# The first attention and routing of a two-layer cross-attention kernel: from steps of 512 tokens to single tiles, and from gathered to scattered expert rows

## The reference

```python
x = x + tanh(g_xattn[0]) * xattn0(layernorm(x), ctx)   # 16 heads of 128, rmsnorm on q and k, softmax over 64 keys
x = x + tanh(g_ffn[0])   * ffn0(layernorm(x))          # 64 experts, 8 per token, plus a shared expert
x = x + tanh(g_xattn[1]) * xattn1(layernorm(x), ctx)   # 16 heads of 16, per-head layernorm on q and k, 48+16 keys
x = x + tanh(g_ffn[1])   * ffn1(layernorm(x))          # 8 experts computed densely, top 2 weighted, plus shared
```

```python
scores = sigmoid(x @ router_weight.T); sc = scores + e_bias
# 8 groups of 8 experts: sum of the two best of each group, best 4 groups kept, best 8 experts in them
topk_w = scores[topk_idx]; topk_w = 2.5 * topk_w / topk_w.sum()
pos = (number of earlier tokens, in order, that chose the same expert)   # kept where pos < 128
buf[e, pos] = x[token]                                  # 64 blocks of 128 rows
y = (silu(buf @ w_gate) * (buf @ w_up)) @ w_down        # 88 inner values
out[token] += y * topk_w
```

## Time and profile before

| | us |
|---|---|
| median of 3 runs (lowest, highest) | 1350.04 (1349.48, 1351.49) |
| profiled execution, its own time | 1348.91 |
| its span, first to last instruction | 1347.2 |
| busy PE, PEld, DVE | 1040.4, 860.9, 714.3 |
| busy ACT, POOL | 428.9, 296.6 |
| mean granted TensorE clock | 0.833 |

### The profile page before, as it was taken

How to read it: one execution, slowest core, us unless ns; L and a number is a source line. 1 busy time by engine, 2 the same in 40 slices (tenths; PEclk the granted TensorE clock), 3 DMA queues, 4 the chain that set the end, 5 groups by cost and what they waited for, 6 DMA issues and landing times. The chain is left out here.

```text
span 1347.2 us, 16347 instructions
## 1 busy us (share of the span) xinstructions
PE 1040.4 (77%) x5301; PEld 860.9 (64%) x5301; DVE 714.3 (53%) x1663; ACT 428.9 (32%) x789; POOL 296.6 (22%) x231
## 2 busy tenths in 40 slices
PE   5989989999766500866775447878879999999997
PEld 3857858678554300755665226564757989899896
DVE  6367586674768896222222488575865424242221
ACT  4555365544623100111111032323252232322321
POOL 0414223133000001788787120120200000000000
PEclk9999999999877655877778666767676999999999
DMA  7004000000001140788886620000000000000001
GB/s 264 3 0 136 1 1 1 0 1 1 0 0 39 42 108 22 168 182 175 170 175 113 191 107 1 2 0 0 0 0 0 1 1 0 0 0 0 0 0 63
DMA packets 59495, 66.39 MB, mean 49 GB/s; under 512 B 5565, under 2 KB 56247, under 8 KB 58679
## 3 DMA queue, kind: packets, MB, share of 16 engines
q1 hardware_dynamic: 45796, 46.52, 11.1%
q0 software_dynamic: 12288, 18.88, 7.9%
q10 hardware_dynamic: 1363, 0.37, 0.1%
HBM read 48.16 MB, written 17.56 MB: 49 GB/s over the span
## 5 line engine op out<-in xcount | busy, mean ns | idle before, releaser
L1978 PE MATMUL bank<-gu_hi,xnT_split 128*128 128x352 f32 x640 | 159.4, 329 | 0.0
L476 POOL TENSOR_TENSOR q_lo<-soft,q_hi 128x512 fp32r<-128x512 f32 x64 | 93.1, 1455 | 238.0 <-ACT soft L1338 237.8
L1978 PEld LDWEIGHTS bank<-gu_hi,xnT_split 128*128 128x128 f32 x640 | 113.4, 191 | 1.0 <-issue 0.7
L487 POOL DMA_INDIRECT xg<-table,src_now x64 | 63.9, 999 | 217.6 <-DVE src_now L948 198.5
L497 POOL DMA_INDIRECT acc<-y,dst_now x64 | 102.2, 1596 | 26.7 <-issue 20.6
L1978 PE MATMUL bank<-gu_lo,xnT_split 128*128 128x352 f32 x320 | 104.2, 326 | 0.0
L1208 DVE SCALAR_TENSOR_TENSOR soft<-sg,combine_w,bank 128x176 f32<-128x176 f32 x160 | 56.5, 394 | 88.1 <-PE bank L1978 82.3
L1997 PE MATMUL bank<-dn,attnT 128*128 128x256 f32 x448 | 102.1, 387 | 0.0
L1997 PEld LDWEIGHTS bank<-dn,attnT 128*128 128x128 f32 x448 | 86.1, 195 | 11.5
L728 DVE COPY qT<-bank 128x512 f32<-128x512 f32 x64 | 44.2, 690 | 89.3 <-PE bank L1683 88.2
L1536 ACT ACTIVATE sg<-bank 128x352 f32<-128x352 f32 x80 | 37.1, 464 | 153.0 <-PE bank L1978 153.0
(11 more groups left out here) (255 smaller groups left out, 2165.4 us busy)
## 6 DMA issues: line engine op xcount, KB each, us to landing
w_gu<-in_L_ffn_w_gu SPq DMA_DIRECT2D x32, 352.0 KB
w_dn<-in_L_ffn_w_down SPq DMA_DIRECT2D x32, 176.0 KB
acc<-zeros SPq DMA_DIRECT2D x2, 2176.0 KB, 12.0
acc_rows<-acc SPq DMA_DIRECT2D x8, 512.0 KB, 4.9
gu<-in_L_gu SPq DMA_DIRECT2D x1, 3520.0 KB, 13.3
table<-xw SPq DMA_DIRECT2D x4, 640.0 KB
wo<-in_L_xattn_Wo SPq DMA_DIRECT2D x2, 1024.0 KB, 15.7
wq<-in_L_xattn_Wq SPq DMA_DIRECT2D x1, 2048.0 KB, 18.0
```

Of the source, the lines that this page charges most:

```text
L476: pool.tensor_tensor(q2_lo[:, h % 3, :], q2[h % 2], q2_hi[:, h % 3, :], ALU.subtract).then_inc(q2_split, 1)
L487: pool.indirect_dma_start(xg[:, q, e, :], None, table, bass.IndirectOffsetOnAxis(ap=src_now[:, q, e:e + 1], axis=0)).then_inc(xg_loaded[q] ...
L1978: mm = pe.matmul(b[:, 0:2 * F1], v[:, c, j * P:(j + 1) * P], w[:, c, p, o, :], start=(n == 0), stop=(n == len(terms) - 1))
```

## The change

The first layer's attention becomes a loop of 18 slots, unrolled, one tile of 128 tokens to a slot. The order of fills of all four PSUM rings is written out by name (`first_stage_turns`, class `Turns`), and each engine looks its position up there.

Queries are now projected with the tile stationary and 512 columns of `wq` moving, and are used for their norms alone: ACT squares each head's 128 columns in PSUM with a sum (`query_norms`). Scores come from the normed tile and a matrix per context batch, a = Wq^T-folded keys: for each head PE multiplies `wqT` by `kT` (`fold`), and ACT lays the result in `a_sk`. Key norms are also squares with sums on ACT (`keys_in`). `raw` holds one tile. Routing runs inside the loop on pairs of tiles (`choose`), five slots behind; the position of a token in its expert's block is a count made by PE with a triangular matrix (`place`); the two instructions' results are row numbers in a DRAM table of 64 x 128 rows. POOL sends each token's row (256 values, 64 weights, its own number) with eight indirect stores a tile (`send_rows`). Blank rows are written to the whole table at the start, with numbers of spare rows in the accumulators. The shared expert runs after the loop. The slot search and the gathers are gone: SP loads blocks with plain DMAs (`load_rows`), and the adding scatter takes its indices from the loaded rows.

In the second attention the centring is done once, on weights and biases (`centre_weights`, placed before the last round of experts), and weight and bias of the per-head norm are applied by ACT in the copies that follow the transposes (`queries1_in`, `keys1_in`). Loads, waits and names follow. The core of the diff, cut:

```diff
+            sp.dma_start(wq[:], a["L0_xattn_Wq"]...).then_inc(wq_loaded, 16)
+            sp.dma_start(wqT[:], a["L0_xattn_WqT"]).then_inc(wqT_loaded, 16)
             sp.dma_start(wvT[:], a["L0_xattn_WvT"]).then_inc(wv_loaded, 16)
+            sp.dma_start(wvo[:], a["L0_xattn_Wo"]...).then_inc(wo_loaded, 16)
             sp.dma_start(x[:, G:NT, :], x_d[:, G:NT, :]).then_inc(x_rest_loaded, 16)
+            for n in range(4):
+                each = E0 // 4
+                sp.dma_start(table_d[:, n * each:(n + 1) * each, :], blank[:].unsqueeze(1).to_broadcast(
+                    [P, each, ROW])).then_inc(blank_stored, 16)
+            for n in range(NA):
+                sp.dma_start(acc[n]..., blank[:, 0:DIM]...).then_inc(zeroed, 16)
+            for g in range(1, NG):
+                sp.wait_ge(t_ring.full, t_turn.at["ctxV", g - 1] + 1)
+                sp.dma_start(ctx_rows[:], ctx_d[g * P:(g + 1) * P, :]).then_inc(ctx_loaded, 16)
...
+            sp.wait_ge(row_stored, 16 * K0 * NT)
+            for q in range(4):
+                load_rows(0, q)
...
                     sp.wait_ge(y_full, 4 * i + q - 3)
                     load_experts(i, q)
+                    for n in range(NA):
+                        sp.wait_ge(acc_added[n], 16 * (4 * i + q - 3))
+                    load_rows(i, q)
```

```diff
+            def send_rows(b):                                  # POOL
+                if b >= 2:
+                    pool.wait_ge(row_stored, 16 * K0 * 2 * (b - 1))
...
+                pool.wait_ge(slots_ready, b + 1)
+                if b == 0:
+                    pool.wait_ge(blank_stored, 16 * 4)
+                for j in range(2):
+                    for k in range(K0):
+                        pool.indirect_dma_start(table, bass.IndirectOffsetOnAxis(ap=slots[:, b % 2, j, k:k + 1], axis=0),
+                                                rows[:, b % 2, j, :], None, bounds_check=E0 * CAP - 1,
+                                                oob_is_err=False).then_inc(row_stored, 16)
-            def gather(i, q):
-                for e in range(2):
-                    pool.indirect_dma_start(xg[:, q, e, :], None, table, bass.IndirectOffsetOnAxis(
-                        ap=src_now[:, q, e:e + 1], axis=0)).then_inc(xg_loaded[q], 16)
```

```diff
+            def slot(i):                                       # DVE
+                if i >= 6 and i % 2 == 0:
+                    place((i - 6) // 2)
+                if i >= 5 and i % 2:
+                    choose((i - 5) // 2)
+                roots(i)
+                if i >= 2:
+                    apply2(i - 2)
+                if i + 1 < NT:
+                    apply1(i + 1)
+                if i < NT:
+                    soft_front(i)
+                if i + 1 < NT:
+                    split1(i + 1)
+                if 1 <= i <= NT:
+                    residual1(i - 1)
+                if i % G == 0 and i // G + 1 < NG:
+                    key_norm(i // G + 1)
+                if i < NT:
+                    soft_back(i)
```

```diff
+            def keys_in(g):                                    # ACT
+                for n in range(4):
+                    b = q_turn.read(act, ("keys", g, n))
+                    act.activation(ksb[:, 4 * n:4 * n + 4, :], b[:]..., ACT.Copy).then_inc(keys_copied, 1)
+                    act.wait_ge(keys_copied, 4 * g + n + 1)
+                    for k in range(4):
+                        v = b[:, k * D0:(k + 1) * D0]
+                        ins = act.activation(v, v, ACT.Square, accum_out=kstat[:, 0, 4 * n + k:4 * n + k + 1])
+                    ins.then_inc(q_ring.free, 1)
+            def slot(i):
+                g = i // G
+                if 1 <= i < NT:
+                    query_norms(i)                             # 16 squares with a sum, like the above
+                if i >= 3:
+                    scores_in1(i - 3)
+                if g and i < NT and i % G == 1:
+                    values_in(g, range(4, 8))
+                if 1 <= i <= NT:
+                    attn_in(i - 1)
+                if i + 1 < NT:
+                    tokens_in(i + 1)
+                if i < NT:
+                    exponential1(i)
+                if i == 0:
+                    product_in()
+                    values_in(0, range(8))
+                if i < NT and g and i % G == 0:
+                    values_in(g, range(2, 4))
+                if g + 1 < NG:
+                    if i % G == 0:
+                        context_in(g + 1)
+                        keys_in(g + 1)
+                    elif i % G == 1:
+                        keysT_in(g + 1)
+                    elif i % G == 2:
+                        fold_in(g + 1, 0)
+                    else:
+                        fold_in(g + 1, 1)
+                        values_in(g + 1, range(2))
+                if i >= 2:
+                    rows_in(i - 2)
```

```diff
+            def slot(i):                                       # PE
+                if 1 <= i < NT:
+                    queries(i)
+                if i >= 3:
+                    route(i - 3)
+                if g and i < NT and i % G == 1:
+                    values(g, range(4, 8))
+                if 1 <= i <= NT:
+                    transpose_attn1(i - 1)
+                if i < NT:
+                    scores1_(i)
+                if i + 1 < NT:
+                    transpose1(i + 1)
+                if 1 <= i <= NT:
+                    output1(i - 1)
+                if i >= 5 and i % 2:
+                    place((i - 5) // 2)
...
-                for h in range(H0):
-                    b = qr.fill(pe)
-                    terms = [(w, v, c) for c in range(C) for w, v in (
-                        (wq_hi, xnT_top), (wq_hi, xnT_rest), (wq_lo, xnT_top))]
```

More of the change, by code:

```diff
@@ L179, in flamingo @@
[L179 to L189, removed]
@@ L490, in scatter @@
+            for b in range(NT // 2):
+                send_rows(b)
+            pool.drain().then_inc(done1["pool"], 1)
             def scatter(i, q):
@@ L827, in _, with two @@
[L827 to L846 removed]
+            def two(v):
+                return v.rearrange("p (j e) -> p j e", j=2)
@@ L954, in experts @@
+            shared_product(0)
+            shared_product(1)
+            place(last)
+            for i in range(NG):
+                if i >= 2:
+                    shared_product(i)
+                shared_out(i)
+            dve.drain().then_inc(done1["dve"], 1)
+            CH1 = ch.base + ch.k
+            for e in done1.values():
+                dve.wait_ge(e, 1)
+            sl = Chain(dve, slot_chain)
+            def experts(i):
                 qr.at(Q3, 4, i)
                 for q in range(4):
-                    if not (last and q):
-                        stage_source(i + (q + 3) // 4, (q + 3) % 4)
@@ L1377, in _ @@
+            for i in range(NT + 2):
+                slot(i)
+            scores_in1(NT - 1)
+            for i in range(NG):
+                if i >= 2:
+                    act.wait_ge(o_ring.full, o_turn.at["shared", G * (i - 2) + G - 1] + 1)
+                act.activation(sh_g[:, i % 2, :], q_turn.read(act, ("gate", i))[0:I0, :], ACT.Silu).then_inc(q_ring.free, 1)
             act.drain().then_inc(done1["act"], 1)
@@ new lines, in scores1_ @@
+            def scores1_(t):
+                if t % 2 == 0:
+                    t_turn.emptied(pe, ("fold", t // G, 1, 3))
+                for n in range(2):
+                    b = s_turn.fill(pe, ("scores", t, n))
+                    for c in range(C):
+                        mm = pe.matmul(b[:], xnT1[:, t % 2, c, :], a_sk[:, (t // 2) % 3, c, n * 512:(n + 1) * 512],
+                                       start=(c == 0), stop=(c == C - 1))
+                    mm.then_inc(s_ring.full, 1)
@@ new lines, in shared_out @@
+            def shared_out(i):
+                s_turn.emptied(pe, ("up", i))
+                for j in range(G):
+                    b = o_turn.fill(pe, ("shared", G * i + j))
+                    pe.matmul(b[:, 0:DIM], sh_h[:, i % 2, j * P:(j + 1) * P], sh_dn[:], start=True,
+                              stop=True).then_inc(o_ring.full, 1)
+            pe.wait_ge(ident_ready, 1)
+            context_in(0)
+            pe.wait_ge(wk_loaded, 16)
+            keys(0)
+            transpose1(0)
```

1368 lines of the change are left out of this document (653 added, 715 removed).

## The result

The changed kernel takes **1376.38 us** (median of 4 runs, 1374.01 to 1385.0), the kernel before 1349.76 in the same comparison: the ratio is 1.0207, with a 95% interval from 1.0162 to 1.0252. It is slower, by 1.6 to 2.5%; I had forecast 1297 with a range of 1235 to 1348. The profiled execution took 1374.01 us with a span of 1372.3.

What follows compares the result with a forecast made beforehand. Bounds: PE to about 335 us, not PE from 335 to 531 (softmax, routing, slot search), POOL in the experts. 1347.2 - 40 (experts ending earlier) - 13 (second attention) = 1294 span, plus 1.7 and 1.1: 1297 us, range 1235 to 1348.

Steps and rivals of the forecast that it cites:

- Then the tail is POOL's: After the slots end at 433 us, POOL's stores of blocks 5, 6 and 7 remain, 21 us a block, 63 us.
- First rows: Start of the experts' stage: first rows at 518 us, where the kernel before has them at about 536.
- Rival (3): POOL's stores are held up or as dear as scatters, 1.93 us: 30 us more in the tail, 1327; chance 0.13.
- A group of four tiles: Expert-free first attention loop: four slots take 103 us, of which PE works 75.
- the 15 us that I had added for clocks and semaphores: Added to 503 us for lower clocks in gaps and semaphores between engines, giving 518 us before the experts.
- The context: Loop's start: next context's load, behind blank rows and zeros on SP's queue, lands at 77 us; 15 us lost.
- Squares with sums: ACT's sixteen squares a tile in the loop, taken at 0.36 us each, bounds 0.17 and 0.47.
- rival (4): ACT becomes the loop's bound, sums at 0.47 us: about 9 us a group, 36 in all, 1333; chance 0.15.
- The stores' own price: Each of POOL's indirect stores priced 1.02 + 0.30 = 1.32 us, with the adding scatter's 1.93 as other bound.
- rival (5): PE's clock falls to mean 0.67 in the loop: about 95 us more, less the 15 counted, 1377; chance 0.12.
- Experts: Expert loop: 5.7 us a pair for 6.4 before, seven us to first scatter, stage ending at 706, 40 less.
- Second attention and mixture: Stages after the experts: second attention gains 8 in group 0 and 5 in the others, mixture unchanged; total 13 less.

Runs made afterwards that it cites:

- e9: The changed kernel with three row buffers in place of two and POOL keeping at most two stores under way: 1306.2 us.
- e2: e1 with the second context's load issued ahead of the blank rows' and zeros' stores on SP's queue: 1353.96 us.
- e8: The changed kernel with three row buffers, early context load, early choose, and POOL keeping at most two stores under way: 1287.69 us.
- e1: The changed kernel with three buffers for rows and slots in place of two, and a store semaphore for each: 1361.58 us.

## Why the prediction was wrong, step by step

- **The step that failed** is "Then the tail is POOL's", with what stands ahead of it: stores were priced in the tail only, and the slots were costed as if the 80 stores beside slots 6 to 15 were nothing to DVE, PE and ACT. First rows came at 587 where I had 518, and 69 of the 79 us between forecast and result are there (the experts' stage has another 9). In its place the runs show two costs of the stores in the slots, DVE's wait for landed rows and the late starts behind PE; with both gone (e9) the kernel is 70 us faster. Rival (3) had stores dear or held up, and no rival had them hold others up.
- **A wait missed in the diff.** apply2's wait on `row_stored` is one of the waits that the change adds, and I didn't name it, nor what stands behind it on DVE. Alone it is not the whole case: removing it gives 15 us as things are, and 119 (1425.6 to 1306.2) once the stores are paced.
- **The slots were costed rightly.** A group of four tiles was to be 103 us. From Exp of slot 4 to Exp of slot 8, and from there to slot 12, it is 126.2 and 126.9 in the changed kernel, 100.2 and 99.6 in e9. The forecast for a loop undisturbed by the stores was good: e9's first rows come at 511.3 (518 forecast), and its 1306.2 us lie 9 from 1297. The tail's part of that is luck: e9's last three blocks of stores take 77 us for the 63 forecast, and the 15 us that I had added for clocks and semaphores cover it.
- **The context.** It was transposed at 78.37 us after a wait of 5.67 on its DMA; I had the landing at 77 but PE's request at 62, and it was 72.7. The 15 us were 5.7 by that wait and 7.6 by e2.
- **Squares with sums, rival (4).** They start 0.28 us apart; I took 0.36, with bounds 0.17 and 0.47. ACT's timeline shows the read of a sum as an instruction of its own, which begins under the end of the square:

```profile
208.80 0.27 ACT L1333 ACTIVATE bank<-bank 128x128 f32<-128x128 f32 x1
208.99 0.18 ACT L1333 ACTIVATION_READ_ACCUMULATOR bank<-bank 128x1 f32 x1
209.08 0.27 ACT L1333 ACTIVATE bank<-bank 128x128 f32<-128x128 f32 x1
```

- **The stores' own price, rival (3).** 0.98 + 0.30 us against 1.32 taken and 1.93 as bound. The Trainium skill (SBUF — State Buffer, Who interferes with whom) lets a VectorE instruction and a GpSimd one block each other, and names descriptor generation as what can be starved. In the changed kernel it doesn't show: of its 128 stores 125 keep 0.98 to 1.01 us, and none meets one of DVE's products of 1024 values with both inputs in SBUF. In e8 some do, and a store that begins beside such a product is longer, up to 1.97 us, and ends some 0.85 us behind it:

```profile
306.92 1.23 DVE L790 TENSOR_TENSOR raw<-raw,sums 128x1024 f32<-128x1024 f32 x1
307.06 1.94 POOL L581 DMA_INDIRECT table<-rows,slots  x1 [0.72 <-issue]
```

  Such a meeting costs POOL up to 1 us and is rare (8 stores of e8's 128 take over 1.05 us, the very first one among them), so the rival's mechanism exists and its 30 us don't. In the other direction, DVE's small instructions mostly keep 0.18 us beside the stores, where the earlier trace rows had 0.97 beside POOL's arithmetic.
- **PE's clock, rival (5).** It gave 1377, which is the result to 1 us, for a reason that was hardly at work. The clock is 0.97 from 100 to 205 us, with the same alternation of PE and DVE; it is 0.83 where PE stands still for other reasons, and e9 has 0.90 over 205 to 503. For nearly the same instructions PE is busy 252.62 us at 0.83 and 236.59 in e9, so the lower clock is worth at most 16 us of the 70 between the two. A number that fits is no proof: the mechanism has to be seen in the trace.
- **Experts and second attention.** 5.93 us a pair ((188.2 - 4.4)/31) for 5.7 taken, 7 us in all, and 2 more between first rows and first scatter (9.15 for 7). The queues of 587 to 785 us show gathers gone from the software queue (32.2% against 49.3% in the earlier trace rows) and their bytes on the hardware queue (47.0% against 25.8%): the engines' sum is about what it was (79% of 198 us are 157, 75% of 215 are 161). Second attention and mixture gave 13 for 13; no run took that part alone, so this rests on the windows.

## What to carry to other kernels

When a change puts a long train of POOL's indirect stores beside a pipeline, cost it on the others' side as well: keep two under way (1288 us here, for 1340 in one train), or wait after every fourth (1293), and check what overwrites the source. For each wait that a diff adds, write down when its releaser starts, in the same timetable as the waiter; here both stood in one slot. And when removing the largest wait of a list moves little, look at the same place in the new trace before looking elsewhere: a second cause can hide under the first.

## What the runs showed of the hardware that I had not expected

While POOL sends indirect stores of 128 rows of 1284 B one after the other, 1.28 us apart, instructions of ACT and DVE that read what PE has written start late. In e1's slot 10 they start 5.6 to 13.3 us after PE's end, one after another and up to 5.7 us apart. Such starts lie between about the sixth store of a block and 3 us after its end. Signals of DVE and ACT to PE were not late. The late starts are gone with two stores under way (1.65 to 1.82 us a store) and with trains of four, and they aren't there with plain stores of the same rows from POOL (0.55 us each) or from SP. Whether the signal leaves PE late or arrives late, and through what, no trace here shows.

The price of an indirect store also depends on DVE: 0.98 us by itself, up to 1.97 us in e8 when it begins beside a DVE product of 1024 values with both inputs in SBUF.
